# A low-rank product whose two instructions per pair change places

## The reference

```
x = x + L0(x)   # x @ w_eff.T, w_eff = a quantized weight plus a rank-64 correction
x = x + L1(x)   # x @ W.T + 2 * sum over experts of gate * (x A_e) B_e, top 2 of 8 experts, rank 16
x = x + L2(x)   # x @ W.T + b + 2 * (x A_s) B_s, rank 16, adapter s chosen by sequence
x = x + L3(x)   # x @ weight[adapter].T, the matrix chosen by sequence
```

## Time and profile before

| | us |
|---|---|
| median of 3 runs | 643.15 (642.81 to 643.3) |
| profiled execution, its own time | 643.43 |
| its span | 641.6 |
| PE busy | 635.9 (99%), 3992 multiplications |
| PEld busy | 588.1 (92%), 3992 loads |
| DVE busy | 501.4 (78%) |
| ACT busy | 365.0 (57%) |
| POOL busy | 92.8 (14%) |

### The profile page before, as it was taken

The page is one execution under the profiler, slowest core; times in us unless marked ns, Lnnn a source line. Parts: engine busy times, 40 slices in busy tenths (PEclk is TensorE's granted clock), DMA queues, the critical chain, the costliest instruction groups (busy, mean ns, idle before and its releaser), DMA issues.

```text
span 641.6 us, 10326 instructions
## 1 busy us (share of the span) xinstructions
PE 635.9 (99%) x3992; PEld 588.1 (92%) x3992; DVE 501.4 (78%) x645; ACT 365.0 (57%) x549; POOL 92.8 (14%) x120
## 2 busy tenths in 40 slices
PE   8999999999999999999999999999999999999997
PEld 8899999999999999998889999889999889999886
DVE  6899999879990539978887878888687889686753
ACT  6764583972731346746773746665645765654553
POOL 2320225003110010001221001231001221000020
PEclk9999999999999999999999999999999999999999
DMA  9672212111103001113673222574213475001462
GB/s 283 211 201 71 62 33 66 34 33 34 34 4 128 1 1 61 47 55 107 208 244 120 66 67 67 199 263 156 66 34 100 154 273 189 1 1 67 129 232 98
DMA packets 46020, 67.32 MB, mean 105 GB/s; under 512 B 3604, under 2 KB 32020, under 8 KB 45972
## 3 DMA queue, kind: packets, MB, share of 16 engines
q1 hardware_dynamic: 40900, 58.28, 28.3%
q10 hardware_dynamic: 5072, 8.39, 3.7%
HBM read 58.27 MB, written 8.39 MB: 104 GB/s over the span
## 4 chain that ended last, share of the span: by engine, by line
PE 92%; DVE 4%; SPq 1%; DMA 1%; POOL 1%; ACT 0%; issue 0%; ACTq 0%; DVEq 0%
PE ps L1261 28%; PE ps L1263 28%; PE ps L1262 28%; PE ps L1404 4%; PE ps L1406 1%; PE ps L1433 1%; DVE tmp L970 1%; DMA e_both_w<-w_t 1%; DVE e_both L899 1%; SPq L410 1%; POOL e_both_w L549 1%; PE ps L1272 1%; SPq L427 0%; DVE w_w L960 0%; DVE w_w L966 0%
## 5 line engine op out<-in xcount | busy, mean ns | idle before, releaser
L1261 PE MATMUL ps<-e_both,ring_hi 128*128 128x384 f32 (+3 forms) x384 | 133.3, 347 | 0.1
L1263 PE MATMUL ps<-e_both,ring_lo 128*128 128x384 f32 (+3 forms) x384 | 133.2, 347 | 0.0
L1262 PE MATMUL ps<-x_both,e_both 128*128 128x256 f32 x448 | 125.3, 280 | 0.0
L899 DVE TENSOR_TENSOR e_both<-raw,e_both 128x512 fp32r<-128x512 f32 x128 | 91.2, 737 | 27.2 <-ACT e_both L773 26.7
L1262 PE MATMUL ps<-e_both,e_mid 128*128 128x512 f32 (+2 forms) x288 | 109.2, 379 | 0.0
L1261 PE MATMUL ps<-e_both,e_mid 128*128 128x512 f32 (+2 forms) x288 | 109.1, 379 | 0.0
L1263 PE MATMUL ps<-e_both,e_mid 128*128 128x512 f32 (+2 forms) x288 | 109.1, 379 | 0.0
L773 ACT ACTIVATE e_both<-raw 128x512 fp32r<-128x512 f32 x128 | 78.8, 628 | 51.5 <-PE ps L1263 51.2
L589 POOL TENSOR_TENSOR raw<-raw,ident 128x128 f32<-128x128 f32 x64 | 45.3, 710 | 345.0 <-DMA raw<-w_t 345.0
L1262 PEld LDWEIGHTS ps<-x_both,e_both 128*128 128x128 f32 x448 | 85.5, 191 | 0.0
L1261 PEld LDWEIGHTS ps<-e_both,ring_hi 128*128 128x128 f32 x384 | 72.2, 188 | 6.0 <-DVE ring_lo L899 0.3
(11 more groups left out here) (175 smaller groups left out, 1289.1 us busy)
## 6 DMA issues: line engine op xcount, KB each, us to landing
raw<-w_t SPq DMA_DIRECT2D x64, 512.0 KB, 4.2
w_w<-x_t SPq DMA_DIRECT2D x16, 512.0 KB, 3.8
w_w<-w SPq DMA_DIRECT2D x15, 512.0 KB, 5.2
y<-tmp ACTq DMA_DIRECT2D x30, 256.0 KB, 3.0
e_both_w<-w_t SPq DMA_DIRECT2D x5, 512.0 KB, 8.0
e_both_w<-w_t SPq DMA_DIRECT2D x4, 384.0 KB, 6.2
e_mid_w<-bs SPq DMA_DIRECT2D x24, 64.0 KB, 2.9
e_mid_w<-b_cat SPq DMA_DIRECT2D x4, 128.0 KB, 6.0
```

What stands on the lines that cost most here:

```text
L899: return dve.tensor_tensor(out, whole, hi.bitcast(F32), ALU.subtract)
L1261: pe.matmul(out, a[0], b_[0], start=start, stop=False, **kw)
L1262: pe.matmul(out, a[0], b_[1], start=False, stop=False, **kw)
L1263: return pe.matmul(out, a[1], b_[0], start=False, stop=stop, **kw)
```

## The change

In each pair of `low_rank` the two multiplications change places. The one with x's low part stationary and 152 moving columns comes first and now carries `start` at k = 0; the one with x's high part and 304 columns comes second and now carries `stop` at k = 7 and, as the last of the group, the increment of `t_done`. Operands, columns, banks, waits and counts are as they were.

```
                     for k in range(KT):
                         block = f"B{k // 4 + 1}{t // 2 + 1}"
-                        pe.matmul(ps[:, 4 + t, 0:2 * TW].rearrange("p (h c) -> p h c", h=2), x_hi[block][:, k % 4, cols],
-                                  e_both[:, k, :, ecols], start=k == 0, stop=False, skip_group_check=True)
-                        ins = pe.matmul(ps[:, 4 + t, 0:TW], x_lo[block][:, k % 4, cols], e_hi[:, k, ecols],
+                        pe.matmul(ps[:, 4 + t, 0:TW], x_lo[block][:, k % 4, cols], e_hi[:, k, ecols],
+                                  start=k == 0, stop=False, skip_group_check=True)
+                        ins = pe.matmul(ps[:, 4 + t, 0:2 * TW].rearrange("p (h c) -> p h c", h=2),
+                                        x_hi[block][:, k % 4, cols], e_both[:, k, :, ecols],
                                         start=False, stop=k == KT - 1, skip_group_check=True)
                 ins.then_inc(t_done, 1)
```

## The result

| | before | after |
|---|---|---|
| median, us | 643.11 (642.81 to 643.3, 4 runs) | 638.87 (638.71 to 639.42, 4 runs) |
| ratio | | 0.9935 (95%: 0.9923 to 0.9947) |
| profiled execution / span | 643.43 / 641.6 | 638.79 / 637.0 |

Forecast was no change, 643.15 with a range of 642.5 to 643.9. Timed again on another occasion, the kernel after gave 638.95 and a ratio of 0.9933 (0.992 to 0.9947).

The account below looks back on a forecast made before the run. The prediction took PE, running without a gap, to bound the kernel, so the distances between its starts make the time. Its terms summed 0 + 0 + 0 + 0, leaving 643.15 us, with a range of 642.5 to 643.9.

Parts of the forecast that it names:

- What bounds the kernel: Whole kernel: PE runs without a gap, busy 635.9 of 641.6 us, so distances between its starts make the time.
- Pace of a pair, inside and from tile to tile: Inside `low_rank`: a pair takes 0.253 us in either order; 31 of a group's 32 pairs cost the same, 0.
- Entry: First pair of `low_rank`, four times: 0.22 us becomes 0.25 on the records, +0.03, taken back at the end of the stage.
- `start`: Opening 16 banks with the narrow multiplication: no price, 0, with ends of -0.2 to +0.2 us.
- Exit: From `low_rank` into the block product, four times: 0.41 us becomes 0.37, -0.04; with the start of `low_rank`, taken as 0.
- The signs that I named: Trace checks: right if `low_rank` stretches last 8.07 to 8.15 us; wrong if pairs take 0.22 or 0.29, or PE waits anew.
- `t_done`: Semaphore increment at the end of `low_rank`: 0.01 to 0.04 us later, hidden in idle time, 0; at most +0.1 us.
- Rival A: Faster: `low_rank` pairs keep 0.22 us throughout instead of 0.253, gaining 4.1 us, so 639.1; chance 4%.
- B: Slower: both loads of each `low_rank` pair exposed, 0.29 us instead of 0.253, +4.5 us, so 647.6; chance 3%.
- C: Slower: opening a bank on the narrow multiplication makes PE pause, 16 x 0.23 = 3.7 us, so 646.8; chance 1%.

Follow-up runs that it names:

- e1: Kernel before with only the last pair of the last tile of each group in the new order; 643.64 us, ratio 1.0005.
- h1: Kernel before, old pair order, plus one 256-column multiplication per group between `low_rank` and the first block product; 639.63 us, ratio 0.9941.
- g4: Kernel after with a 64-column multiplication ahead of every second chunk of the second fold step; 641.1 us in its one execution, span 638.3.
- e3: Kernel before plus one 304-column multiplication per group between `low_rank` and the first block product, sum thrown away; 644.12 us.
- f3: Kernel before plus one multiplication of 256, 288, 384 or 512 columns (groups 0 to 3) between `low_rank` and the first block product; 640.05 us.

## Why the prediction was wrong

- *What bounds the kernel* held: PE without a gap, the sum of its distances is the time.
- *Pace of a pair, inside and from tile to tile* held: `low_rank` is 8.10 to 8.11 us, inside the 8.07 to 8.15 I named, with 0.07 and 0.18 alternating. I took the swing of a few ns for rounding; it was there at 1 ns.
- *Entry* was right: the first wide one is noted 0.07 behind the narrow one and takes 0.18; *`start`* too, 0.18 and 0.07 at k = 0 as elsewhere. The exit's own distances were right as well: 0.37 us from the last narrow one to the second 256, as worked out.
- *Exit* is the step that failed, in what it leaves out. It says of the 256-column multiplication that it "takes its usual 0.12" and stops counting at the second of them; the sum has no term for the 240 behind, which puts their change at nothing without a reason. The usual 0.12 was no price of the instruction but one of two paces, 117.8 and 113.3 ns, and what runs ahead chooses which the following 240 get: 960 x 4.6 ns = 4.4 us. I set bounds of 0.2 us for this step from the two starts next to it, and asked nowhere how the stage behind reacts. The signs that I named looked only at the changed stage too: those for "right" came true there but for one of 0.01 us, none of those for "wrong" did, and the forecast was wrong all the same. The row that would have warned me was in the trace of before, as shown above: the same instructions at 113 ns.
- *`t_done`*: in group 1 line 810 starts 0.19 behind the block product's first start (345.82 against 345.63); before it was 0.20. I expected 0.00 to 0.05 more. The difference is below what matters, and it brings nothing: e1 has `t_done` on a wide one and no gain, h1 has it on a narrow one and most of the gain.
- *Rival A*, at 4%, named 639.1 for a pair of 0.22, and 638.87 was measured. That the time is near is luck: no pair got quicker, the 4.1 us of A would have come from `low_rank`, and `low_rank` grew by 0.13. *B* and *C* did not occur.
- The Trainium skill's page "TensorE: Matmul & The Clock Gate", section "LDWEIGHTS (loading the stationary operand)", puts a load for 128 columns at 107 ns. An estimate: at the full clock that was granted here, 2.4 GHz, 256 columns stream in 256 / 2.4 = 107 ns as well. Both paces measured, 113.3 and 117.8 ns, lie above that, so it explains neither. That load and stream are so nearly equal is a reason to suspect them, and no run here separates the two. Other widths were hardly tried: only in g4's fold (384, 392 and 512 columns), where no second steady pace showed.

**Open.** What the two paces are inside the engine, and by what the exchange of the pairs picks the fast one. Shown is that there are two, that they last to the end of the 240, that one instruction moves the run between them, and that none of pair order, exit width, `t_done` and the order of k decides by itself; nor does the sequence of widths (h1). That it is a phase between loads and streams is argued: in ns, a load starts 2 to 5 behind its forerunner's multiplication at the slow pace and 3 to 4 at the fast one, and the multiplication 114 to 115 behind its load at the slow one and 110 at the fast one. Which phases lead where was not mapped. All extra multiplications behind `low_rank` went to another bank than the tile's own, e3's moved E where f3's and h1's moved x, and none of this was varied by itself.

## What to carry to other kernels

A long run of equal multiplications may have more than one steady pace; here that is shown for 256 columns. Count starts in equal stretches across stages that do the same thing; if one is 4% denser, it is worth trying a small change ahead of the slow one (here one 256-column multiplication of 0.16 us bought 1.1 us in each group). The fold holds a candidate that no run tried: its chunk of 24 256-column multiplications from 124.08 in after takes 2.82 us, 117.7 ns each. And an edit that costs nothing by its own rows can still move what runs behind it: before a forecast of "no change", look whether the following stage has shown another pace elsewhere in the trace.

## What was not expected of the hardware

The two paces are 117.8 and 113.3 ns in every group and kernel. They repeat in every profiled execution, and the times say the same of the others: 10 executions of e1 lie between 643.21 and 644.17, 9 of after between 638.71 and 639.6. The recorded length of the multiplication tells them apart at once, 281 ns at the slow pace and 276 at the fast one (means over a stretch of group 0, before and then after; columns as on the page):

```profile
L1262 PE MATMUL ps<-x_both,e_both 128*128 128x256 f32 x69 | 19.4, 281 | 0.0
```

```profile
L1262 PE MATMUL ps<-x_both,e_both 128*128 128x256 f32 x71 | 19.6, 276 | 0.0
```

Having a multiplication with 96 rows as every fourth, rather than four together behind twelve, cost the gate stage 5.5 ns on each of its 64 (0.35 us in all). Whether it is the 96 rows or the other change of operands that costs it was not varied.
